# Four single PSUM banks, handed out oldest first, in place of two slots of two banks

## The reference

```python
x = L0_attn_x                                           # (2, 1024, 128)
x = _layernorm(x + _L0_attn_ref(x, ...))                # retention, 8 heads, decay, gated
x = _layernorm(x + _L0_ffn_ref(x, ...))                 # causal attention, 16 heads of 8, then 4 experts, one per token
x = _layernorm(x + _L1_attn_ref(x, ...))                # full attention, 16 heads of 8
x = _layernorm(x + _L1_ffn_ref(x, weight))              # ternary weights, 128 x 128
```

```python
scores = jnp.einsum('bhqd,bhkd->bhqk', q, k) / np.sqrt(HEAD_DIM)
attn = jax.nn.softmax(scores, axis=-1)
out = jnp.einsum('bhqk,bhkd->bhqd', attn, v).transpose(0, 2, 1, 3).reshape(b, t, D_MODEL)
```

```python
top = jnp.argmax(logits, axis=-1)
onehot = jax.nn.one_hot(top, N_EXPERTS, dtype=x.dtype)
h = jax.nn.relu(jnp.einsum('btd,ehd->bteh', x, W1) + b1)
y = jnp.einsum('bteh,edh->bted', h, W2) + b2
```

## Time and profile before

| | |
|---|---|
| three runs, us | 1009.87, 1010.62, 1011.01 |
| median | 1010.62 us |
| profiled execution, first to last instruction (span) | 1007.3 us |
| median less span | 3.3 us |
| PE busy | 883.9 us, 88% |
| DVE busy | 764.2 us, 76% |
| ACT busy | 654.5 us, 65% |
| POOL busy | 390.2 us, 39% |

### The profile page before, as it was taken

How to read it: one execution, slowest core, us unless ns; L and a number is a source line. 1 busy time by engine, 2 the same in 40 slices (tenths; PEclk the granted TensorE clock), 3 DMA queues, 4 the chain that set the end, 5 groups by cost and what they waited for, 6 DMA issues and landing times.

```text
span 1007.3 us, 22853 instructions
## 1 busy us (share of the span) xinstructions
PE 883.9 (88%) x9093; PEld 447.3 (44%) x9098; DVE 764.2 (76%) x1156; ACT 654.5 (65%) x1285; POOL 390.2 (39%) x607
## 2 busy tenths in 40 slices
PE   7999999998878888888988678889989999999983
PEld 5778777787633443334562222236322222222232
DVE  4667766856587677887667498786889999999855
ACT  2555565655526777785546548775768988998881
POOL 3755767778332551124454211352341112111340
PEclk8999999999899999998998899999999999999996
DMA  8000000200501034111420601033106000100000
GB/s 299 1 2 1 1 1 2 75 1 1 151 1 41 22 131 139 39 39 49 133 75 2 202 21 40 4 98 105 52 2 202 21 20 20 30 11 2 4 23 22
DMA packets 49407, 52.53 MB, mean 52 GB/s; under 512 B 8875, under 2 KB 40619, under 8 KB 49141
## 3 DMA queue, kind: packets, MB, share of 16 engines
q1 hardware_dynamic: 45012, 48.12, 15.6%
q0 software_dynamic: 4288, 2.94, 1.1%
HBM read 32.37 MB, written 19.68 MB: 52 GB/s over the span
## 4 chain that ended last, share of the span: by engine, by line
PE 49%; DVE 29%; ACT 7%; issue 5%; DMA 4%; POOL 3%; SPq 2%; DVEq 0%; ACTq 0%; POOLq 0%
DVE arena L1956 21%; PE banks L1618 9%; PE banks L1583 7%; PE banks L1503 5%; ACT arena L1776 3%; PE banks L759 3%; PE banks L485 3%; PE banks L495 2%; PE banks L1693 2%; PE banks L1701 2%; DMA arena<-arena 2%; PE banks L654 2%; PE banks L754 1%; PE banks L716 1%; PE banks L705 1%
## 5 line engine op out<-in xcount | busy, mean ns | idle before, releaser
L1776 ACT ACTIVATE arena<-banks 128x512 f32<-128x512 f32 (+1 forms) x768 | 409.1, 587 | 115.3 <-PE banks L1583 81.9
L1956 DVE TENSOR_REDUCE arena<-banks 128x2 f32<-128x1024 f32 (+1 forms) x384 | 440.1, 1198 | 56.3 <-PE banks L1503 29.1
L1618 PE MATMUL banks<-arena 128*9 128x256 f32 (+1 forms) x3328 | 252.6, 379 | 7.4 <-ACT arena L1789 4.6
L1503 PE MATMUL banks<-arena 56*128 56x512 bf16 (+3 forms) x896 | 163.3, 366 | 31.8 <-DVE arena L1956 25.2
L1583 PE MATMUL banks<-arena 61*128 61x512 bf16 (+4 forms) x896 | 165.5, 369 | 28.7 <-ACT arena L1776 20.9
L1583 PEld LDWEIGHTS banks<-arena 61*128 61x128 bf16 (+1 forms) x896 | 44.7, 93 | 185.3 <-ACT arena L1776 155.5
L1357 POOL CAST arena<-arena 16x128 bf16<-16x128 f32 x32 | 8.9, 279 | 296.2 <-ACT arena L1844 292.3
L1618 PEld LDWEIGHTS banks<-arena 128*9 128x9 f32 x3328 | 51.9, 89 | 130.7 <-issue 82.4
L1503 PEld LDWEIGHTS banks<-arena 56*128 56x128 bf16 x896 | 45.2, 95 | 57.1 <-DVE arena L1956 44.6
L383 POOL TENSOR_TENSOR arena<-arena 128x8 f32<-128x8 f32 (+1 forms) x35 | 51.3, 1467 | 30.7 <-DVE arena L2120 28.3
L1367 POOL DMA_DIRECT2D arena<-arena x96 | 55.1, 577 | 10.7 <-POOL arena L1360 9.2
(11 more groups left out here) (243 smaller groups left out, 1460.5 us busy)
## 6 DMA issues: line engine op xcount, KB each, us to landing
arena<-k_products SPq DMA_DIRECT2D x32, 224.0 KB
arena<-q_products SPq DMA_DIRECT2D x64, 112.0 KB
q_products<-arena SPq DMA_DIRECT2D x16, 384.0 KB, 3.4
k_products<-arena SPq DMA_DIRECT2D x16, 384.0 KB, 3.8
arena<-e_w SPq DMA_DIRECT2D x22, 256.0 KB, 3.3
arena<-arena POOLq DMA_DIRECT2D x96, 4.0 KB, 1.8
sorted_rows<-c_pads SPq DMA_DIRECT2D x2, 709.5 KB, 8.5
arena<-sorted_rows SPq DMA_DIRECT2D x4, 258.0 KB, 3.0
```

What stands on the lines that cost most here:

```text
L1503: ins = nc.tensor.matmul(bank(first + par)[:, at:at + hi - lo], Qs[k_][rows, qc, y, qo:qo + P], Ks[k_][rows, y, lo:hi], start=True, stop=n ...
L1618: ins = nc.tensor.matmul(PS[h * VROWS:h * VROWS + VW, AV_BANK, o:end], V[:, b, kt, HG * g + h, :], Pr[u % PROBS][:, h, o:end], start=(kt = ...
L1776: s_.activation(Pr[s % PROBS][:, 2 * x + par, o:C], scores[:, o:C], ACT.Exp) \
L1956: v_.tensor_reduce(of[:, :, x], two_banks[:, :, 0:width], AX.X, ALU.max).then_inc(ring_dve, 1)
```

## The change

The four banks are handed out one by one. A scan or an "h" (`wide`) takes the pair (2, 3) or (0, 1) whose younger holder is the older of the two; every other entry takes the one bank whose holder is oldest. `before[r]` lists the entries that hold those banks, and PE waits for exactly these. If several are listed it waits on both drain counters. No entry changes its place in the list on any engine, and no product, reduction or transfer is added or taken away.

```diff
-        RING = (2, 0)
+        BANKS = 4
...
+        wide = [e[0] == "h" or e[0] == "A" for e in ring]
+        home, before = [], []
+        held = [None] * BANKS
+        for r in range(len(ring)):
+            age = [-1 if u is None else u for u in held]
+            if wide[r]:
+                first = min((2, 0), key=lambda q: max(age[q:q + 2]))
+            else:
+                first = min((2, 3, 0, 1), key=lambda q: (age[q], -age[q ^ 1]))
+            span = range(first, first + 1 + wide[r])
+            home.append(first)
+            before.append(sorted({held[q] for q in span if held[q] is not None}))
+            for q in span:
+                held[q] = r
...
-        def emptied(eng, r):
-            if ring[r][0] not in BY_ACT:
-                eng.wait_ge(ring_dve, by_dve[r])
-            if ring[r][0] in BY_ACT or ring[r][0] in BY_BOTH:
-                eng.wait_ge(ring_act, by_act[r])
+        def emptied(eng, items):
+            of_dve = [by_dve[r] for r in items if ring[r][0] not in BY_ACT]
+            of_act = [by_act[r] for r in items if ring[r][0] in BY_ACT or ring[r][0] in BY_BOTH]
+            if of_dve:
+                eng.wait_ge(ring_dve, max(of_dve))
+            if of_act:
+                eng.wait_ge(ring_act, max(of_act))
...
             def ring_bank(r):
-                return RING[r % len(RING)]
+                return home[r]
...
-                        if r >= len(RING):
-                            emptied(pe, r - len(RING))
+                        emptied(pe, before[r])
```

More of the change, by code:

```diff
@@ L1161, in build @@
         place = {e: r for r, e in enumerate(ring)}
+        wide = [e[0] == "h" or e[0] == "A" for e in ring]
[12 more added lines that the diff above has]
+                held[q] = r
+        opened = {}
+        for r, first in enumerate(home):
+            for q in range(first, first + 1 + wide[r]):
+                opened.setdefault(q, r)
         by_dve = list(accumulate(int(e[0] not in BY_ACT) for e in ring))
         by_act = list(accumulate(int(e[0] in BY_ACT or e[0] in BY_BOTH) for e in ring))
-        def emptied(eng, r):
-            if ring[r][0] not in BY_ACT:
-                eng.wait_ge(ring_dve, by_dve[r])
-            if ring[r][0] in BY_ACT or ring[r][0] in BY_BOTH:
-                eng.wait_ge(ring_act, by_act[r])
+        def emptied(eng, items):
[5 more added lines that the diff above has]
+                eng.wait_ge(ring_act, max(of_act))
         def taken(eng, kind, k):
-            emptied(eng, place[kind, k])
+            emptied(eng, [place[kind, k]])
         def scored(m):
@@ L1460, in _ @@
                         bk = bank(ring_bank(r))
-                        if r >= len(RING):
-                            emptied(pe, r - len(RING))
[L1463 to L1466, removed]
+                        emptied(pe, before[r])
+                        for q in (q for q, u in opened.items() if u == r):
+                            pe.wait_ge(o_kept if q >= 2 else g_silu, NTILE)
                     if kind == "D16a":
```

## The result

The changed kernel takes 999.34 us (four runs, 996.77 to 1002.50), the kernel before 1010.82 us beside it (four runs, 1009.87 to 1012.59). The ratio is 0.9888, 95% interval 0.9861 to 0.9916: 11.5 us faster, where 4.8 were forecast. The sign and the places were right; the size was not.

A forecast was written before the change was run, and what follows sets the result against it. No engine is full throughout; PE and DVE wait for each other in turn. Savings of 5.60 us less 0.3 and 0.5 make 4.8 us, 1010.6 to 1005.8 us; range 1001.8 to 1009.6, 8 times in 10.

The forecast's parts named there:

- eleven places: Spots where a second close small entry waited for the younger scan; its earlier release saves 0.19 to 0.77 us each.
- slower: Rival: half-clock stretches shift to where PE is full, 485 to 520 us; three new ones cost 5.1 us; chance 0.06.
- absorbed: Rival: the next wait, on ACT or the DMA, takes up the savings; time 1009.6 us; chance 0.20.
- signs of being wrong: ACT's or DMA's waits grown by DVE's loss, half-clock stretches changed by three, or first entries at 265 to 270 us mattering.
- the sum 5.60 us: Total saving forecast over the eleven places, before deductions, mostly from PE's idle time ahead of each second small entry.
- K 2: Small entry behind O 0, near 320 us; waits for A(19, 0) in place of A(19, 1), saving 0.47 us.
- Q 3: Another second small entry released earlier, the same way as K 2; saving 0.77 us.
- KL 3: Second small entry; PE gains 0.48 us, DVE stood only 0.17 us before its next scan; 0.30 us taken.
- The 0.3 us for added waits: Cost of up to 45 more stand-alone waits of 51 ns on PE's weight-load queue; between 0 and 2.3 us.
- The 0.5 us lost to later waits: Deduction for savings partly lost where the DMA of the maxima or ACT ends the next wait.
- The other entries at nothing: Some twenty more entries with earlier releases, but no PE idle time ahead or waiting for data; costed at 0 us.
- The clock: Rival: denser work lifts half-clock stretches at 465.50 and 646.40 us, up to 1.7 us each; 1002.4 us; chance 0.17.

The follow-up runs named there:

- the run with the old waits: Changed kernel's banks, but each entry also waits, as before the change, for the entry two places back; 1009.96 us, ratio 1.0008 to the kernel before.
- Four comparisons: Single banks at the eleven places only against the changed kernel, plain twice (0.9878/0.9858, 0.9922/0.9884), with twenty unused products once (0.9927/0.9914); all but the eleven against before, 0.9984.
- the two with filled waits: Old waits kept, unused products put into them: pairs for all, eight places, 1015.55 us (0.9973); changed kernel's banks, eleven places, 1018.5 us (0.9979).
- either part of them alone: Against the kernel before, single banks only at K 2, Q 3 and KL 3: 1015.70 us (0.9966); only at the other eight places: 1012.54 us (0.9936).

## Why the prediction was wrong

**What held.** The reading of what bounds the kernel: PE waiting for DVE at the second of two close small entries. The run with the old waits shows that the whole gain passes through the waits. All eleven places gain, their brackets are gone where the rows were shown, the scan waits stayed (52 after 48), the full stretch is unchanged and only earlier, stand-alone waits are 151. Of the rivals, *slower* and *absorbed* didn't come: ACT's waits are 19.5 us after 18.9, the DMA's 3.4 after 5.8. One of the prediction's signs of being wrong did come, half-clock stretches fewer by three: up to the last layer there are fourteen of 3.4 us in the profile before and eleven after, though two of the three lie in the first layer, whose code is the same. The sentence on PSUM double buffering that the prediction quotes for the absorbed case from the Trainium skill, "TensorE: Matmul & The Clock Gate", section "HAM oscillation — how this bites in real kernels", doesn't carry over to a kernel whose idle time was ended by a drain.

**The size of the eleven places.** The step that failed first is the sum 5.60 us. It took PE's idle bracket as the saving. Measured are 7.5 us (table; 7.7 by the fit). The bracket runs from the drawn end of the product ahead to the start of the next, and products overlap when nothing holds them back, 0.07 us at K 2 and 0.16 at Q 3. The Trainium skill, "Perfetto Trace Analysis", section "Tensor Engine Instruction (MATMUL, LD_WEIGHTS)", says that a product's end in the profile is computed from its size and not observed; by this case's rows it lies up to 0.16 us behind the point from which the next could start. The better measure was in the same rows: DVE's idle time before its next reduction, 1.36 and 1.78 us, of which 0.54 and 1.04 went. For KL 3 I took 0.30 because DVE had only 0.17 us to give. DVE stood another 0.19 us before the scan behind that one (at 359.82 us), and in the changed kernel both brackets are gone:

```profile
359.82 1.23 DVE L1956 TENSOR_REDUCE arena<-banks 128x2 f32<-128x1024 f32 x1 [0.19 <-PE banks L1513]
354.30 2.35 DVE L1972 TENSOR_REDUCE arena<-banks 128x2 f32<-128x1024 f32 x2
```

The first row is the kernel before, the second the changed one. The entries filled from there on are 0.67 us earlier. A neighbour that is busy delays a saving and doesn't end it, if it is idle soon after.

**The deductions.** The 0.3 us for added waits could not be seen: the run with 164 stand-alone waits is level with the kernel before, which has 110 of them (1.0008, 0.9989 to 1.0026). The 0.5 us lost to later waits was not lost by the table.

**The other entries at nothing.** Some twenty entries were costed at nothing, with PE's own work as cover. Four comparisons give them 1.3 to 3.9 us, most with an interval that nearly or fully reaches zero, and on average about 2. Which of these entries carry it is not shown.

**The clock.** I had it as a rival of its own, up to 3.4 us at two stretches, in place of a part of every case. PE busy in the old waits makes the kernel 2.1 and 2.7 us faster on two chips at a granted clock higher by 0.004. The two stretches of the earlier trace rows are only in part where it came from: the one behind G 1 is gone, but that behind G 0 lies at 466.0 to 472.8 us after the change, twice as long. One other place shows in the profiles, between K 2 and G 0. The old waits and the changed kernel, both on the third chip:

```profile
298.50:450.00 151.50, 130.57 (x1879) 56.44 (x1881) 119.44 (x151) 108.68 (x237) 51.32 (x96) 0.99 0.23 68
298.50:450.00 151.50, 132.04 (x1965) 58.27 (x1965) 122.39 (x155) 111.49 (x243) 55.33 (x100) 1.00 0.23 69
```

The first has a stretch at half clock from 346.0 to 349.4 us. All seven profiles that keep the old waits at K 2, Q 3 and KL 3 have at least one between 298.5 and 450 us, the two with filled waits too; of the eleven with these waits released nine have none. For the rest only the sum over a run is shown. The sentence of the Trainium skill, "TensorE: Matmul & The Clock Gate", section "A second HAM failure mode: psum-queue depth-cycling", on small idle gaps, which I gave to this rival, agrees with this in kind: fewer short waits went with a higher clock where all were released, 0.9712, 0.9714 and 0.9648 after 0.9650, 0.9658 and 0.9610, but hardly with either part of them alone.

**The sum.** 7.5 us at the eleven places, about 2 at the others, about 2.5 by the clock make 12. The changed kernel was measured four times, at 0.9888, 0.9858, 0.9876 and 0.9884, on average 12.5 us. The first part is firm. How the other 5 us divide between other entries and the clock is known to about a microsecond, and only if the fit's two assumptions hold; by single comparisons to a microsecond or two.

No version was faster than the changed kernel by more than can be told.

## What to carry to other kernels

Price a released wait by what the engine behind stands idle (DVE's bracket before its next reduction), or by the start-to-start distance of the same two operations where nothing holds them; PE's own bracket is too small by the overlap of products. When close small items share a ring with large ones, look at which item a wait really names: handing out the oldest free bank removed 7.5 us here without moving an instruction. If the matrix engine's granted clock falls in places, add to every saved stall a gain of its own, here about a quarter to a third of the direct one, and widen the range for it.

## What the hardware showed that was not expected

- PE filled with unused products during waits that stay made the kernel faster, 0.9973 (0.9952 to 0.9994) and 0.9979 (0.9956 to 1.0003, an interval that ends at no change); filled for longer than the wait lasts it made it slower, 0.9914 against 0.9876 (the intervals just overlap; 4.3 us by the fit).
- A microsecond more at half clock went with 0.2 to 0.3 us more of the kernel's time, not the half that a PE-bound stretch would give. That DVE and ACT bound part of such stretches is a likely reason and not shown.
- A stand-alone wait whose count is already there takes 51 ns on PE's weight-load queue; 54 more of them could not be seen in the time.
- One and the same kernel took 1009.4 to 1020.4 us on four chips, while its executions on one chip lie within some 1% of each other.
